# Pairwise products of projected features on one core: the last feature of the last tile loaded ahead of its tile, in fifteen short transfers

## The reference

```python
_I, _J = np.triu_indices(40, k=1)
proj = jnp.einsum('bnd,ed->bne', x, W)
out = proj[:, PAIR_I, :] * proj[:, PAIR_J, :]     # 512 x 780 x 128, float32
```

## Time and profile before

| | |
|---|---|
| median of 3 runs | 504.46 us (504.24 to 504.70) |
| the profiled execution | 504.4 us |
| its span, first to last instruction | 502.6 us |
| VectorE busy | 432.0 us, 86% |
| TensorE, ScalarE busy | 63.2 us, 54.1 us |
| moved by DMA | 215.12 MB, mean 428 GB/s |

### The profile page before, as it was taken

How to read it: one execution, slowest core, us unless ns; L and a number is a source line. 1 busy time by engine, 2 the same in 40 slices (tenths; PEclk the granted TensorE clock), 3 DMA queues, 4 the chain that set the end, 5 groups by cost and what they waited for, 6 DMA issues and landing times.

```text
span 502.6 us, 1469 instructions
## 1 busy us (share of the span) xinstructions
PE 63.2 (13%) x481; PEld 57.6 (11%) x481; DVE 432.0 (86%) x188; ACT 54.1 (11%) x162; POOL 0.7 (0%) x6
## 2 busy tenths in 40 slices
PE   1999990000000000000000000000000000000000
PEld 1988890000000000000000000000000000000000
DVE  0899999999999999999999889999999998999900
ACT  1788880000000000000000000000000000000000
POOL 0000000000000000000000000000000000000000
PEclk9999996555555555555555555555555555555555
DMA  8999999999999999999999999999999999999998
GB/s 354 427 442 424 435 424 418 448 413 449 416 448 413 451 420 448 416 448 416 448 416 448 416 448 416 445 423 442 426 439 426 432 430 432 432 432 432 432 432 359
DMA packets 6487, 215.12 MB, mean 428 GB/s; under 512 B 720, under 2 KB 848, under 8 KB 848
## 3 DMA queue, kind: packets, MB, share of 16 engines
q1 hardware_dynamic: 6336, 214.96, 99.4%
q10 hardware_dynamic: 144, 0.07, 0.0%
HBM read 10.55 MB, written 204.47 MB: 428 GB/s over the span
## 4 chain that ended last, share of the span: by engine, by line
DMA 55%; DVE 37%; DVEq 1%; PE 1%; issue 0%; ACT 0%
DMA out_dram<-products 53%; DVE products L196 37%; DMA w_in<-in_L_rec_W_dram 2%; DVEq L54 1%; PE proj_ps L131 1%; PE turned_ps L122 0%; PE w_ps L140 0%; ACT feats L174 0%
## 5 line engine op out<-in xcount | busy, mean ns | idle before, releaser
L196 DVE TENSOR_TENSOR products<-feats 128x1664 f32<-128x1664 f32 (+32 forms) x188 | 432.0, 2365 | 45.6 <-DMA out_dram<-products 30.7
L131 PE MATMUL proj_ps<-w_turned,x_turned 128*128 128x128 f32 x320 | 55.0, 296 | 0.8 <-ACT x_turned L168 0.7
L131 PEld LDWEIGHTS proj_ps<-w_turned,x_turned 128*128 128x128 f32 x320 | 43.5, 197 | 5.3 <-ACT x_turned L168 1.9
L122 PE MATMUL turned_ps<-identity,feats 128*128 128x128 f32 x160 | 31.5, 284 | 1.4 <-ACT feats L174 1.4
L174 ACT COPY feats<-proj_ps 128x256 f32<-128x256 f32 x80 | 29.8, 372 | 10.3 <-PE proj_ps L131 5.0
L168 ACT COPY x_turned<-turned_ps 128x256 f32<-128x256 f32 x80 | 29.9, 378 | 2.2 <-PE turned_ps L122 2.0
L122 PEld LDWEIGHTS turned_ps<-identity,feats 128*128 128x128 f32 x160 | 20.9, 148 | 2.3 <-ACT feats L174 2.0
L140 PE MATMUL w_ps<-identity,w_in 128*128 128x128 f32 x1 | 0.4, 443 | 10.5 <-DMA w_in<-in_L_rec_W_dram 10.5
L164 ACT ACT_TABLE_LOAD x1 | 1.3, 1283 | 1.2 <-PEq L211 1.2
L140 PEld LDWEIGHTS w_ps<-identity,w_in 128*128 128x128 f32 x1 | 0.2, 182 | 10.4 <-issue 10.4
L164 ACT COPY w_turned<-w_ps 128x128 f32<-128x128 f32 x1 | 0.3, 265 | 8.5 <-PE w_ps L140 8.5
## 6 DMA issues: line engine op xcount, KB each, us to landing
out_dram<-products SPq DMA_DIRECT2D x40, 4992.0 KB, 24.6
feats<-in_r_x_dram SPq DMA_DIRECT2D x4, 2560.0 KB, 17.9
w_in<-in_L_rec_W_dram ACTq DMA_DIRECT2D x1, 64.0 KB, 9.6
```

The source lines that it names most:

```text
L122: last = pe.transpose(turned_ps[group % 2][:, n - a, :], feats[:, tile, n, :], identity[:, :])
L131: last = pe.matmul(proj_ps[group % 2][:, k, :], x_turned[group % 2][:, k, :], w_turned[:, :], start=True, stop=True)
L196: last = dve.tensor_tensor(products[c % SLOTS][:, place:place + count, :], feats[:, tile, i:i + 1, :].broadcast_to([P, count, DIM]), feats ...
```

## The change

The loads of tiles 0, 1 and 2 stay. Of tile 3, feature 39 alone (512 B in each partition) is loaded first, in fifteen transfers that take 15, 14, 13, ... 3, 2 and 9 of the 128 partitions in turn. Then one transfer brings features 0 to 38 of all 128 partitions, 19,968 B each. All sixteen raise `tiles_loaded`, and TensorE's one wait for it counts fifteen transfers more. Nothing else differs; the lines below it in the file move down.

```diff
+PARTS = list(range(15, 1, -1)) + [9]
+assert sum(PARTS) == P
...
             sp.dma_start(feats[:, 0, :, :], x[0:P, :, :]).then_inc(first_loaded, 16)
-            for tile in range(1, tiles):
+            for tile in range(1, tiles - 1):
                 sp.dma_start(feats[:, tile, :, :], x[tile * P:(tile + 1) * P, :, :]).then_inc(tiles_loaded, 16)
+            last, row = tiles - 1, 0
+            for rows in PARTS:
+                sp.dma_start(feats[row:row + rows, last, FEATURES - 1, :],
+                             x[last * P + row:last * P + row + rows, FEATURES - 1, :]).then_inc(tiles_loaded, 16)
+                row += rows
+            sp.dma_start(feats[:, last, 0:FEATURES - 1, :],
+                         x[last * P:(last + 1) * P, 0:FEATURES - 1, :]).then_inc(tiles_loaded, 16)
...
-            pe.wait_ge(tiles_loaded, 16 * (tiles - 1))
+            pe.wait_ge(tiles_loaded, 16 * (tiles - 1 + len(PARTS)))
```

## The result

The changed kernel takes 505.29 us (median of 15 runs, 505.22 to 505.65), the kernel before 504.28 us in the runs beside it (503.99 to 504.70). The ratio is 1.0021 with a 95% interval of 1.0014 to 1.0028: slower by 1.0 us, at the very edge of what I had called no change (503.5 to 505.5). The profiled execution took 505.31 us with a span of 503.5, so again 1.8 us lie around the span and the loss is inside it.

What follows compares the result with a forecast made beforehand. The prediction took DMA bytes over rate as the bound: 214.96 MB at 432.5 GB/s, 497.0 us. It added only 0.14 us for short packets to 504.4, giving 504.5 us, own range 503.9 to 505.2, outer range 502.9 to 505.7.

Steps and rivals of the forecast that it cites:

- no change: Whole kernel: likeliest case, 503.5 to 505.5 us, about what a measurement cannot tell apart; chance 0.69 with rival 4 included.
- the issues on SyncE: Loads of the last tile: sixteen issues in place of one, the last out at 11.4 us; cost 0.
- the wait of TensorE: Before the second tile: passes when the last load lands, up to 0.7 us later; cost 0.
- the rate in the long middle: Stores from 100 to 455 us: stays at 432 to 433 GB/s; one GB/s of movement is 0.8 us.
- the outer range: Whole kernel: range that leaves out 2 in 10, from 502.9 to 505.7 us.
- The sum: Whole kernel: 504.4 + 0 + 0.14 + 0 + 0 = 504.5 us; 0.14 is half the mean engine's +0.28.
- the rate from 4 to 26 us: Loads: sign that the rate stays within 2 GB/s of its value before.
- rival 1: Stores: DMA engines out of step run faster and end together, 1.7 us gained, 502.7 us; chance 0.18.
- the price of the short packets: Last tile's load: at most 0.054 us per row and completion; busiest engine +0.66 us, mean +0.28, empty -0.15.
- Rival 2: Last tile's load: short transfers stall an engine; at 0.2 us each the busiest is 2.5 us late, 506.9; chance 0.10.
- Rival 4: End of the kernel: the busiest engine is also the last one, +0.66 us, 505.1; no chance of its own.
- Its estimate by the ceiling: Stores: 204.5 MB at 435.2 GB/s against 432.5, given as 3.0 us less, 501.4 us; part of rival 1.

## Why the prediction was right in its range and wrong in a step

Right: the issues on SyncE and the wait of TensorE cost nothing, the queue carried the 128 rows and 128 completions counted ahead, the rate in the long middle stayed at 433, and the outer range, 502.9 to 505.7, held the time. The likeliest case was "no change", and 505.29 lies inside the bound given for it, though the interval leaves no doubt that the kernel is slower, and it lies outside that case's own range of 503.9 to 505.2. The sum put the cost at 0.14 us and it was 1.0. That the range held is in part luck: the mechanism was one that I gave 0.10, and it fell on an engine with 9 to 12 short transfers; with 16 on it, in sixteen transfers of 8 rows, the time was 506.10.

One of the signs named ahead said so: the rate from 4 to 26 us was to stay within 2 GB/s of 432, and was 416. The 431 GB/s of 60 to 100 us, called there a sign of rival 1, came with a longer time.

The step that failed is the price of the short packets, 0.054 us for a row and its completion, at most. It was read from the busy share of the queue that loads w, and the packets themselves are as cheap as that, or cheaper. But a share of busy time says how long a packet was on record, not what it does to the packet behind it. The slowed engine has 9 to 12 short transfers. Its load was to end 9 to 12 x 0.054 - 0.15 = 0.3 to 0.5 us later; it began its first store 1.1 us later, and before the change it had waited for that store, as most engines had, by some 0.2 to 0.3 us (from under 0.1 to 0.45 us on those that waited). So its load ended some 1.3 to 1.4 us later, and with the 0.15 us of bytes that it was spared, that is 0.13 to 0.17 us for each transfer, an estimate. The row of w could not show it: those packets alternate with long ones of the other queue, and there is one completion on each engine.

Rival 2, a stall of 0.1 us or more per transfer, was therefore the mechanism, with 0.2 us named as its price and 0.10 as its chance. Its argument against, that the load went at 432 GB/s through every handover between tiles, holds for one completion behind eight long packets and says nothing on many in a row.

Rival 4 was right in kind: the time is set by one engine. But it is not the busiest, if transfers use the lowest engines each time. I took half of the mean engine's load as the cost because "which of these sets the end, the page doesn't tell". The landing times of the 16 shares do tell that a few engines leave the crowd between 40 and 90 us, as long as TensorE works and instructions are fetched; I read the 427 GB/s of 60 to 100 us as a slow stretch of all engines. Of rival 1 the gain exists (435 and 431 GB/s in the stretches to 100 us) and goes to the fifteen engines that don't set the end. Its estimate by the ceiling comes to 2.9 us, not 3.0; nothing rests on it.

Open: why many short transfers stall the packets behind them, and why TensorE's or ScalarE's work slows one DMA engine and no other. No run here separates those causes. That leaving the work out does not shorten the kernel before has a reason in part: in its trace one engine falls 1.0 us back at a fetch of 8 KB at 412.9 us and lands 0.6 us behind the next. The others take 1,482 ns a packet from 100 us on, where the kernel before has 1,481. So in the kernel before the slowed engine ends within 0.2 us or so of the last one, and a delay of it is paid in full beyond that.

## What to carry to other kernels

When 16 engines work a queue down to its end, the time is that of the last one. A change that gives some engines more needs the question which engine is last and what slows it; the mean rate can rise while the time does. Price a short transfer by what the long packets behind it lose, not by the busy time of its own packets, and gather rows in one transfer where it can be done: 128 rows in one transfer cost 0.1 us, which is within the noise, the same rows in fifteen transfers 1.0.

## What the runs showed of the hardware

- A run of short transfers stalls the long packet behind it: up to 1.3 us on a packet of 39,936 B that takes 1.49 us otherwise, up to 1.0 us on each of the first two of 19,968 B. Between 15 and 30 transfers the cost grew from 1.0 to 3.35 us, and short packets themselves then took up to 202 ns in place of 27.
- While TensorE and ScalarE worked, one of the 16 DMA engines needed 1,540 to 1,590 ns for nearly all of 26 to 28 packets in a row, where most others took 1,476 to 1,491.
- In the kernel before, a fetch of 16 KB of instructions took 0.9 to 1.1 us of one DMA engine, and the store packets ahead of it and behind it up to 0.6 and 0.4 us more than usual.
- An issue of 127 rows and one of 1 took 19.33 us together on SyncE; fifteen with 128 rows in all took 5.90.
